# Seventeen constant matmuls in place of twelve at one place of TensorE's order, and none in place of four at another

## What is computed

```python
x = x + _L0_xattn_ref(_layernorm(x), ctx_1024, ctx_1024, ...)      # 16 heads, 154 context tokens
x = x + _L0_ffn_ref(_layernorm(x), ...)                            # 8 experts, each picks 128 of 1024 tokens
x = x + _L1_xattn_ref(_layernorm(x), ctx_1024, mask, W_attn)       # one head, masked
x = x + _L1_ffn_ref(_layernorm(x), Wr, br, ...)                    # 32 experts, top 8, and a shared one
```

```python
def _L1_xattn_ref(dec_out, enc_out, enc_mask, W_attn):
    attn = jnp.einsum('bqd,bkd->bqk', dec_out, enc_out)
    attn = jnp.where(enc_mask, -jnp.inf, attn)
    attn = jax.nn.softmax(attn, axis=2)
    context = jnp.einsum('bqk,bkd->bqd', attn, enc_out)
    cat = jnp.concatenate([context, dec_out], axis=2)
    return jnp.einsum('bqf,af->bqa', cat, W_attn)
```

## Time and profile before

| | before |
|---|---|
| median of 3 runs | 281.58 us (281.22 to 281.99) |
| the profiled execution's own time | 282.88 us |
| its span, first to last instruction | 281.1 us |
| mean granted clock of TensorE | 0.961 |
| TensorE matmul busy | 245.8 us (87%) |
| VectorE, ScalarE, GpSimd busy | 180.1, 133.4, 72.5 us |

### The profile page before, as it was taken

The page is one execution under the profiler, slowest core; times in us unless marked ns, Lnnn a source line. Parts: engine busy times, 40 slices in busy tenths (PEclk is TensorE's granted clock), DMA queues, the critical chain, the costliest instruction groups (busy, mean ns, idle before and its releaser), DMA issues.

```text
span 281.1 us, 3672 instructions
## 1 busy us (share of the span) xinstructions
PE 245.8 (87%) x1244; PEld 168.1 (60%) x1244; DVE 180.1 (64%) x416; ACT 133.4 (47%) x268; POOL 72.5 (26%) x103
## 2 busy tenths in 40 slices
PE   8886998989987666999999768788879999999993
PEld 3454545455644213678788537666558888888872
DVE  3695445363455886677245173688888888888883
ACT  2544364645632940252434233766555555555551
POOL 4572060920305300000192030030023535353200
PEclk9999899999999797799999986999999999999998
DMA  7980000000000000000043000000002121210001
GB/s 244 426 336 3 2 0 0 1 2 1 2 0 0 0 0 2 1 0 0 2 92 100 0 0 0 2 0 1 0 2 61 51 71 44 75 39 0 2 0 75
DMA packets 5156, 11.52 MB, mean 41 GB/s; under 512 B 809, under 2 KB 1929, under 8 KB 4882
## 3 DMA queue, kind: packets, MB, share of 16 engines
q1 hardware_dynamic: 4290, 10.47, 11.3%
q10 hardware_dynamic: 848, 0.82, 0.9%
HBM read 10.77 MB, written 0.52 MB: 40 GB/s over the span
## 4 chain that ended last, share of the span: by engine, by line
PE 65%; DVE 16%; issue 7%; ACT 6%; POOL 5%; DVEq 0%; ACTq 0%; POOLq 0%
PE bank L1517 5%; PE bank L1521 5%; PE bank L1518 5%; PE bank L1047 4%; PE bank L1122 3%; DVE att L571 3%; PE bank L1550 3%; PE bank L1393 3%; PE bank L1066 3%; DVE smax L474 3%; PE bank L1403 3%; PE bank L1547 3%; PE bank L1166 2%; PE bank L1530 2%; PE bank L1548 2%
## 5 line engine op out<-in xcount | busy, mean ns | idle before, releaser
L1012 ACT ACTIVATE arena_d<-bank,bias 128x512 f32<-128x512 f32 x34 | 23.4, 688 | 32.9 <-PE bank L1521 32.9
L868 ACT ACTIVATE arena_c<-bank 128x512 f32<-128x512 f32 x40 | 23.0, 598 | 23.0 <-PE bank L1153 22.9
L474 DVE TENSOR_REDUCE smax<-bank 128x8 f32<-128x1232 f32 x16 | 22.8, 1439 | 15.6 <-PE bank L1122 15.6
L736 DVE SCALAR_TENSOR_TENSOR arena_d<-bank,bias,arena_d 128x512 f32<-128x512 f32 x34 | 25.5, 750 | 10.3 <-ACT arena_d L1012 10.0
L1517 PE MATMUL bank<-arena_b 128*128 128x512 f32 x68 | 27.0, 397 | 0.3 <-DVE arena_d L745 0.3
L1521 PE MATMUL bank<-arena_b 128*128 128x512 f32 x68 | 26.6, 390 | 0.0
L1518 PE MATMUL bank<-arena_b 128*128 128x512 f32 x68 | 26.5, 390 | 0.0
L391 POOL CAST arena_b<-rec 128x512 fp32r<-128x512 f32 x17 | 13.7, 808 | 48.7 <-PE bank L1550 48.6
L297 POOL TENSOR_TENSOR rstd<-vareps,neghalf 128x4 f32<-128x4 f32 x8 | 8.1, 1010 | 62.5 <-DVE vareps L433 62.5
L750 DVE TENSOR_TENSOR arena_a<-arena_d,arena_a 128x512 fp32r<-128x512 f32 x34 | 23.4, 689 | 0.7 <-ACT arena_a L1019 0.7
L633 DVE TENSOR_SCALAR arena_a<-bank,pack 128x512 fp32r<-128x512 f32 x16 | 12.0, 751 | 17.0 <-PE bank L1385 16.9
(11 more groups left out here) (247 smaller groups left out, 517.9 us busy)
## 6 DMA issues: line engine op xcount, KB each, us to landing
rec<-in_rec SPq DMA_DIRECT2D x17, 257.0 KB, 2.7
arena_d<-in_fc SPq DMA_DIRECT2D x1, 2048.0 KB, 11.0
fc<-in_fc SPq DMA_DIRECT2D x1, 2048.0 KB, 15.3
x<-in_x SPq DMA_DIRECT2D x2, 256.0 KB, 4.5
out<-x SPq DMA_DIRECT2D x2, 256.0 KB, 2.0
pack<-in_pack ACTq DMA_DIRECT2D x1, 382.0 KB, 5.0
ctx<-in_ctx ACTq DMA_DIRECT2D x2, 154.0 KB, 8.4
watt<-in_watt SPq DMA_DIRECT2D x1, 256.0 KB, 4.1
```

The source lines that it names most:

```text
L474: dve.tensor_reduce(smax[:, n, :].rearrange("p (q h) -> p q h", q=2), heads(flat[:, c0:c0 + NBLK * P]), AX.X, ALU.max).then_inc(Z["max_don ...
L736: dve.scalar_tensor_tensor(to[:, k % 2, :], bank[:, 2 + k % 2, :], bias[:, u % SPLITS, 1:2], sil[:, k % 2, :], ALU.add, ALU.mult).then_inc ...
L868: act.activation(pT[:, n % RING, :], bank[:, 3 + n % 2, :], ACT.Exp, scale=float(DH) ** -0.5)\
L1012: act.activation(sil[:, k % 2, :], bank[:, k % 2, :], f, bias=bias[:, STEPS[k][0] % SPLITS, 0:1])\
```

## The change

Two numbers in TensorE's order: behind the turns of the scattered halves there are 17 constant matmuls in place of 12, and the four behind the second half's context part are gone.

```diff
                     ins = turn(bank[:, b, i * P:(i + 1) * P], xnT[:, (b * TB + i) * P:(b * TB + i + 1) * P])
                 ins.then_inc(Z["back_psum"], 1)
-            idle_work(12, 5)
+            idle_work(17, 5)
...
             exponents_turned(1)
             context_part(1)
-            idle_work(4, 5)
             ffn_input_turned(0)
             router_logits(0)
             gate_and_up(0)
```

## The result

The changed kernel took 283.33 us in the median of 20 runs (280.39 to 290.0), the kernel before 280.49 us in the median of 20 (278.51 to 284.07). The ratio after to before is 1.0074, with a 95% interval of 1.0046 to 1.0102: some 2 us slower. By the medians it is 2.8 us. The ratios here compare the runs that lie within 1.5% of their kernel's fastest, the medians all runs. The first three runs of the kernel before, whose median was 281.58, stood 1.1 us above the 20.

A forecast was written before the change was run, and what follows sets the result against it. The end was taken to wait for TensorE alone for some 5 us from 167.98, at 1.2 GHz in place of 2.4. Terms 0 - 2.43 + 0 = -2.43 us took 281.58 to 279.2 us, range 278.4 to 283.3.

The forecast's parts named there:

- The five matmuls cost nothing on the path: Behind the scattered halves' turns: five more take 1.08 us within 1.36 us of idle time, 0.28 us to spare; cost 0.
- The third rival: At half 0's turns: the five matmuls push them, at most 1.08 us on one turn, hidden; no chance given.
- They take the fall at the cross scores away, -2.43 us: From half 0's cross scores to half 1's turns: clock stays at 1.00, three groups save 2.43 us.
- first rival: At the cross scores: fall delayed, or absent from the timed runs; 280.7 to 282.4 us in both forms, chance 0.31.
- The four's own time is off the path, 0: Behind the second context part: removing their 1.03 us gains 0, as the FFN input's turns come at ScalarE's pace.
- They don't hold the clock, 0: At the FFN's start: without the four the clock likeliest stays up, cost 0; ends kept at 0 and 3.4 us.
- The second rival: At the FFN's start: clock falls in the thin stretch the four filled, costing 1.7 to 3.4 us; chance 0.22.
- The sum: Whole kernel: 0 - 2.43 + 0 = -2.43 us, taken to the timed runs' median of 281.58, giving 279.2 us.

The follow-up runs named there:

- repetition 1: The kernel before, unchanged, profiled a second time (also called the repetition of the kernel before): one execution, 280.04 us with a span of 278.2.
- 17 and 4: Against the kernel before, 17 constant matmuls in place of 12, the four behind the context part kept: median 283.07 us, 282.4 before, ratio 1.0004.
- the kernel with the four ahead: Against the kernel before, 17 in place of 12, and the four moved ahead of the second context part: median 283.13 us, 281.93 before, ratio 1.0073.
- the eight: Eight constant matmuls in place of the four behind the context part; with 17 in place of 12: median 280.3 us, 281.93 before, ratio 1.0001.

## Why the prediction was wrong

*The five matmuls cost nothing on the path.* Right. They ended 0.28 us before the turns, as worked out, and from the scatter's turns to the first cross scores it took 7.16 us after (166.52 - 159.36) and 7.15 in the repetition of the kernel before (167.45 - 160.30). The third rival, that they push the turns, didn't come.

*They take the fall at the cross scores away, -2.43 us.* Wrong as a term of the sum. The size of one such fall was right: 5.66 - 3.32 = 2.34. But it stood in one of three profiles of the kernel before, and in one of the five profiles of kernels with 12. With 17 matmuls it still came in two of the eight profiles of kernels with 17, the changed one among them, each time for 3.4 us and 1.6 us of time (4.97 - 3.32 = 1.65 after). And 17 and 4 against 12 and 4 measured 1.0004. A third of 2.34 us, an estimate out of three profiles, is some 0.8 us to win on average, and no run shows that it was won. The prediction's first rival had named this: the profiled execution was 1.30 us slower than the median of the first runs, and it was read as if it were the typical one. The Trainium skill, "TensorE: Matmul & The Clock Gate" (Part 1: The HAM clock gate, What's actually happening), says that the monitor doesn't start anew with the kernel, so that the point at which the clock changes differs between runs. Three profiles of the same kernel agree as far as they go: the fall came at the cross scores in one and behind the second half's logits in two.

*The four's own time is off the path, 0.* Right: without them the segment from the second cross scores to the first logits was 13.61 us in the changed kernel, as before.

*They don't hold the clock, 0.* **This is the step that failed.** I kept 0 and 3.4 as ends, took 0 "since the context part ahead is dense and the dense work behind starts 3 us later", and the cost was 2.6 to 2.8 us in each of four profiles. The second rival, with its mechanism, place and price (1.7 to 3.4), was what happened, and I gave it 0.22. The prediction's own count of the thin stretch had pointed there: 1.18 of 2.80 us busy, "much like the stretches that came ahead of the two falls". I set it aside for the dense context part ahead, and that was the reading that misled, since it took dense work by its busy time. In the kernel with the four ahead, the row that led to a fall was busy for 3.08 of 4.10 us, three quarters, most of it the context part; in repetition 1 of the kernel before, TensorE was busy for 2.18 of 3.00 from 181.4 to 184.4 (the row above), and the clock held. Over the same 3.00 us ahead of its fall the first had 2.21. So busy time doesn't tell these two cases apart. Why the context part didn't hold the clock and the four did stays open: it multiplies on 77 of the 128 rows (77*128 in the row ahead of the eight), which no run varied by itself. The expectation that the dense work behind comes soon enough was wrong as well: the clock fell 0.8 us before the first logits after the change, and 1.1 to 1.5 us before them in the three others.

*The sum.* -2.43 + 0 was forecast; by the segments it is +2.6 to +2.8 at the FFN, less what little the five save at the cross scores. The ratio of 1.0074 on 280.5 us is +2.1 (1.3 to 2.9), the medians differ by 2.8. The sum also started too high: from 281.58, the median of three runs, where 20 gave 280.49. From 280.49 the second rival's prices give 282.2 to 283.9, and the measured 283.33 lies inside that as well, so its hit doesn't hang on the start.

## What to carry to other kernels

Before a filler is taken out because its own time is hidden, ask what the clock does at the next dense work on the path, and look at several profiles: a row that says "1.00" with the filler there says nothing about the clock without it. A dip in one profile is a sample, so weigh its price with the share of executions that show it, and compare kernels by segments between fixed instructions, where an effect of 2.7 us stands out that a total hides, when its first 160 us alone vary by 8 us. A fall of the clock is worth a filler only where the end of the program waits for TensorE; the one behind the second half's logits cost nothing in seven profiles.

## What the runs showed of the hardware that was not expected

The same program, on the same data, had its TensorE at 1.2 GHz in different places from one execution to the next, and its total varied from 278.51 to 284.07 us over the 20 runs of the kernel before. Part of that is the load of `in_ind`, for which ScalarE's cast began at 12.96, 15.88 and 18.44 us in the three profiles of that kernel. Seven of the 14 profiles had a stretch at 0.50 that began between 164 and 188; in those seven none began from 196 to 204, and the seven others all had one of 3.4 us that began there. Four matmuls of 1.03 us together, behind the second context part, decided whether the clock was 0.50 or 1.00 over the start of the FFN, for 6.8 us; the same four 3.35 us earlier (6.30 - 2.95) did not.
